# Layer 3 of a graph network: SyncE fetches one gathered column in forty-four, row by row

## The chip, the cores and the metric

The kernel runs on one core of one Trainium2 chip. The metric is the device time of one execution in microseconds. A core has four compute engines: TensorE (PE in the rows), VectorE (DVE), ScalarE (ACT) and GpSimd (POOL). A fifth engine, SyncE (SP), here only issues transfers and waits. A "q" behind a name, as in SPq, is that engine's instruction queue.

## The reference

Four graph layers run on the same graph: 3125 nodes of 64 features and 53125 edges. Each layer normalizes the features, computes something per edge from the features of its two ends, and adds it up per node. The change is in the last layer, called layer 3 here:

```python
Wh = h @ W + b
Wr = Wh[row]
Wc = Wh[col]
dot = jnp.sum(Wr * Wc, axis=-1)
sim = dot / jnp.maximum(nr * nc, EPS)      # nr, nc: the norms of Wr and Wc
prop_pos = jax.ops.segment_sum((base * relu(sim))[:, None] * Wc, row, num_segments=n_nodes)
prop_neg = jax.ops.segment_sum((base * -relu(-sim))[:, None] * Wc, row, num_segments=n_nodes)
return scale * (coeff[0] * prop_pos + coeff[1] * prop_neg + coeff[2] * Wh)
```

So each edge needs one row of a table that holds `Wh` and its norm for every node. The row is chosen by an index that is only known on the device, since the kernel sorts the edges itself.

## The kernel before

Edges and one marker entry per node (56320 places with padding) are sorted by node and laid out as 128 partitions x J = 440 columns. The columns form NBLK = 10 blocks of TB = 44. One indirect gather on GpSimd brings one column: 128 rows, one per partition, each row 130 float32 values (520 bytes) of the table `tab3`. This takes 44 gathers for a block and 440 for the layer.

`gather_blocks` (the indirect DMA is L831) issues them in order. The rows go into a ring of two slots (`ring.rows`, RING = 2). Block b uses slot b % 2. Before it refills a slot, GpSimd waits on `freed[s]`, which VectorE raises at L2835 when it has used the rows for the last time. Each gather adds 16 to the semaphore of its slot. `pieces` lists the parts that the other engines work on, with the semaphore and the count that each must reach: blocks 0 to 8 whole, then block 9 in three pieces of 24, 12 and 8 columns (LAST).

In `layer3_gather`, ScalarE waits for a part to be complete and turns its rows into a bank (`turn_rows`, L2771). VectorE runs a segmented scan over it (L2813), forms the similarities and weights (L2817 to L2832), multiplies the rows by them (L2834), frees the slot and scans again (L2837). ScalarE then packs the sums (L2784, semaphore `packed`). SyncE's whole duty in this phase is one store for each part after `packed` (L2754). ScalarE waits for the store of one part before it packs the next whole block, as there is a single buffer `sums`. `layer3_tail` then collects the sums with 25 more gathers (L2866).

The phase begins when `tab3` has been stored. SyncE does this in seven groups in `layer2_tail` (L2465), after ScalarE has finished each (`tabled`). Early in the same function VectorE rewrites the edge indices `by_src.other` as offsets into the table, counted in float32 values (L2613 to L2617).

Addresses in registers are used elsewhere in the kernel. The helper `values` (L1874) loads one or more integers from on-chip memory into an engine's registers. At L1811 SyncE uses one such value as the start of a 128-partition transfer, inside a loop of layer 1. At L1829 to L1831 TensorE's queue loads two lists of 12 values for each step.

Other transfers of SyncE whose rows are used: L1099 (97 rows of 512 bytes, on a queue that had been idle for longer than a microsecond), L1658 (67 single values, right behind L1657), L2298 and L2299 (12 rows of 512 bytes each into one partition), L2300 (one row of 512 bytes into one partition), L2190 to L2192 (64 rows of 256 bytes each), L685 (3200 single values).

Of the kernel before, what the change touches and what calls it, by code (L numbers as in the profile page):

```python
# [13 lines left out]
F32 = mybir.dt.float32  # L14
BF16 = mybir.dt.bfloat16
I32 = mybir.dt.int32
# [4 lines left out]
P = 128  # L21
N = 3125
E = 53125
NT = 25
NP = NT * P
# [6 lines left out]
TB = 44  # L32
NBLK = J // TB
RING = 2
# [15 lines left out]
R3 = 2 * (D + 1)  # L50
R3N = 3 * (D + 1)
# [28 lines left out]
SIDE = NBLK  # L80
CARRY_AT = (2, 4)
NORMED = 3


class Kern:
# [22 lines left out]
def build(nc, a, out):  # L108
    top = ExitStack()
    with top:  # L110
        K = Kern()
        K.nc, K.a, K.out = nc, a, out
        K.semaphores, K.gathers = [], []

        def sb(n, s, d=F32):
            return top.enter_context(nc.sbuf_tensor(n, s, d))

        def dram(n, s, d=F32):
            return nc.dram_tensor(n, s, d, kind="Internal").ap()


        K.ident = sb("ident", [P, P])
        K.x = sb("x", [P, NT, D])
        K.hn = sb("hn", [P, NT, D])
        K.by_src = Order("s", sb, dram)
        K.by_dst = Order("d", sb, dram)
        K.meta = sb("meta", [P, J, 2], I32)
        K.st = sb("st", [P, D])
        K.nodes = sb("nodes", [P, J])
        K.keepc = sb("keepc", [CP, SORT_W])  # L130
        K.nxc = sb("nxc", [CP, 1])
        K.nmc = sb("nmc", [CP, 2])
        K.node0c = sb("node0c", [CP, 1], I32)
        K.nodec = sb("nodec", [CP, SORT_W])
        K.base = sb("base", [P, J])
        K.co = sb("co", [P, 5])
        K.co_parts = sb("co_parts", [P, 8])
        K.item_out = sb("item_out", [1, BODIES, IBW], I32)
        K.body_w = sb("body_w", [1, BODIES], I32)
        K.item_slot = sb("item_slot", [1, BODIES, IBW], I32)  # L140
        K.item_first = sb("item_first", [1, BODIES], I32)
        K.srct = sb("srct", [P, J], I32)
        K.cid = sb("cid", [P, SORT_W], I32)
        K.pcol = sb("pcol", [P, 1], I32)
        K.iot = sb("iot", [P, NP])
        K.sums0 = dram("sums0", (L, D))
        K.sums2 = dram("sums2", (L, D))
        K.sums3 = dram("sums3", (L, D))
        K.rowsd = dram("rowsd", (P, J, RE), I32)
        K.recp = dram("recp", (L, RE), I32)  # L150
        K.pairs = dram("pairs", (SORT_L,), I32)
        K.share = dram("share", (NP,))
        K.tab1 = dram("tab1", (NP, R1))
        K.tab2 = dram("tab2", (2 * NP, R2))
        K.tab3 = dram("tab3", (NP * R3N // R3, R3))
        K.tab3n = K.tab3.rearrange("a b -> (a b)").rearrange("(n r) -> n r", r=R3N)
        K.g1 = dram("g1", (P, J, D + 1))

        with Phase(K, "ep") as ph:
            K.rows = EdgeRows(ph)  # L160
            with Phase(K, "first") as first:
                K.first = FirstList(first)
                sort_sources(K)
                layer0_pass(K)
            layer0_finish(K)
            with nc.sbuf_tensor("F", [P, H, SORT_W], F32) as K.F, \
                    nc.sbuf_tensor("item_rel", [P, ITEMS], F32) as K.item_rel, \
                    nc.sbuf_tensor("sel", [P, 4, ITEMS], F32) as K.sel:
                with nc.sbuf_tensor("atp", [P, J, 2 * H], F32) as K.atp, Phase(K, "l1g") as rows:
                    K.l1 = SourceRows(rows)  # L170
                    layer1_gather(K)
                    layer1_softmax(K)
                remaining_edges(K)
                with nc.sbuf_tensor("acc", [P, ACC_W, D + 1], F32) as K.acc, Phase(K, "l1t") as tail:
                    T = Layer1Tail(K, tail)
                    with nc.sbuf_tensor("item_ex", [P, H, ITEMS], F32) as K.item_ex:
                        layer1_spread(K, T)
                        layer1_sums(K)
                    layer1_tail(K, T)
            with nc.sbuf_tensor("wh", [P, NT, R3], F32) as K.wh:  # L180
                with Phase(K, "l2o") as ph:
                    T = Layer2Tail(K, ph)
                    layer2_gather(K, T)
                    layer2_tail(K, T)
                with Phase(K, "l3o") as ph:
                    T = Layer3Tail(ph)
                    layer3_gather(K, T)
                    layer3_tail(K, T)
# [628 lines left out]
    return bass.ds((it * size + s) * TB, TB)  # L817


def gather_blocks(nc, pool, ring, table, index, ready, last=None, axis=0):  # L820


    for b in range(NBLK):
        s, it = b % ring.size, b // ring.size
        ready(b, s, it)
        pool.sem_inc(ring.begun, 1)
        for j in range(TB):
            landed = ring.gathered[s]
            if last is not None and b == NBLK - 1:
                landed = [sem for (c, n), (sem, base) in zip(LAST, last) if c <= j < c + n][0]  # L830
            nc.gpsimd.indirect_dma_start(  # L831
                out=ring.rows[:, s, j, :], out_offset=None, in_=table,
                in_offset=bass.IndirectOffsetOnAxis(ap=index(b, s, j), axis=axis)
            ).then_inc(landed, 16)


def pieces(ring, last):

    whole = [(b, 0, TB, ring.gathered[b % RING], ring.base[b % RING] + (b // RING + 1) * TB * 16) for b in range(NBLK - 1)]
    return whole + [(NBLK - 1, c, n, sem, base + n * 16) for (c, n), (sem, base) in zip(LAST, last)]  # L840


# [1579 lines left out]
def layer2_tail(K, T):  # L2422


    nc = K.nc
    by = K.by_dst
    with Phase(K, "l2t") as ph:
        sel = ph.sb("sel", [P, NP])
        nmb = ph.sb("nmb", [P, D])
# [14 lines left out]
        made, crossed, carry, kept, joined = ph.sems("made", "crossed", "carry", "kept", "joined")  # L2444
        averaged, turned, moved, first, acted, second = ph.sems("averaged", "turned", "moved", "first", "acted", "second")
        spread, rooted, normed, turned3, moved3, third = ph.sems("spread", "rooted", "normed", "turned3", "moved3", "third")
        added, summed, tabled, stored = ph.sems("added", "summed", "tabled", "stored")
        K.tab3_stored = (stored, NG * 16)
        carry_banks = [ph.ps(f"carried{i}") for i in range(2)]
        wh = K.wh  # L2450
        C1 = D + 1
        with Step(nc, pool_ahead=True) as block:
# [7 lines left out]
            @block.sync  # L2460
            def _(sp):
                rows = lambda t: t.rearrange("(w p) r -> p w r", p=P)
                for g, (w, n) in enumerate(GROUPS):
                    sp.wait_ge(tabled, g + 1)
                    sp.dma_start(rows(K.tab3n[:, 0:R3])[:, w:w + n, :], wh[:, w:w + n, :]).then_inc(stored, 16)  # L2465
                sp.wait_ge(*K.tab3_stored)
# [128 lines left out]
            def _(dve):  # L2595
                v = nc.vector
# [18 lines left out]
                v.tensor_scalar(K.by_src.node0n[:, :], K.by_src.node0[:, :], float(R3N), None, ALU.mult)  # L2615
                v.drain()
                v.tensor_tensor(other[:, :], whole[:, 0:J], whole[:, J:2 * J], ALU.add)  # L2617
                v.drain()
                wide = lambda c, ws, n: c[:, ws].unsqueeze(2).to_broadcast([P, n, D])
                def average(t):  # L2620
                    w, n = GROUPS[t]
# [85 lines left out]
def layer3_gather(K, T):  # L2707

    nc = K.nc
    C1 = D + 1  # L2710
    with Phase(K, "l3g") as ph:
# [13 lines left out]
        blank, got, spread, masked, scanned, packed, cut_masked = ph.sems(  # L2725
            "blank", "got", "spread", "masked", "scanned", "packed", "cut_masked")
        last = [ph.gather_sem(f"last{i}") for i in range(len(LAST))]
        freed = [ph.sem(f"freed{s}") for s in range(RING)]
        out = K.sums3.rearrange("(p j) d -> p j d", p=P)
        parts = pieces(ring, last)  # L2730

        def cut(t, f, n):
            return t[:, 0:f * (n + 1)].rearrange("p (f j) -> p f j", f=f)
# [4 lines left out]
        with Step(nc, pool_ahead=True) as block:  # L2738
            @block.gpsimd
            def _(pool):  # L2740
                pool.wait_ge(*K.tab3_stored)
                nc.gpsimd.indirect_dma_start(out=first[:, :], out_offset=None, in_=K.tab3,
                                             in_offset=bass.IndirectOffsetOnAxis(ap=K.by_src.node0n[:, 0:1], axis=1)).then_inc(got, 16)
                def ready(b, s, it):
                    if it:
                        pool.wait_ge(freed[s], it)

                gather_blocks(nc, pool, ring, K.tab3, lambda b, s, j: K.by_src.other[:, b * TB + j:b * TB + j + 1], ready, last, axis=1)

            @block.sync  # L2750
            def _(sp):
                for i, (b, c0, n, landed, count) in enumerate(parts):
                    sp.wait_ge(packed, i + 1)
                    sp.dma_start(out[:, b * TB + c0:b * TB + c0 + n, :], sums[:, c0:c0 + n, :]).then_inc(stored, 16)  # L2754

            @block.scalar
            def _(act):
# [6 lines left out]
                def turn_rows(i):  # L2764
                    b, c0, n, landed, count = parts[i]
                    act.wait_ge(landed, count)
                    if i > SIDE:
                        act.wait_ge(packed, SIDE)
                    elif i and i != SIDE:
                        act.wait_ge(packed, i)  # L2770
# [20 lines left out]
            def _(dve):  # L2791
# [9 lines left out]
                for i, (b, c0, n, landed, count) in enumerate(parts):  # L2801
# [11 lines left out]
                    v.tensor_tensor_scan(flat(whole), keep, flat(whole), 0.0, ALU.mult, ALU.add)  # L2813
                    v.drain()
                    dve.wait_ge(landed, count)
                    v.tensor_copy(q[:, :], whole[:, :, n])
                    v.tensor_tensor(prod[:, 0:n, :], by_entry(whole[:, 0:D, 1:]), r[:, :, 0:D], ALU.mult)  # L2817
                    v.tensor_tensor(nn[:, 0:n], whole[:, D, 1:], r[:, :, D], ALU.mult)
# [146 lines left out]
```

## Time and profile before

| | us |
|---|---|
| median of 3 runs | 3093.05 |
| lowest, highest | 3091.59, 3096.49 |
| the profiled execution, span from first to last instruction | 3095.7 |
| GpSimd busy | 2190.4 (71%) |
| VectorE busy | 1326.6 (43%) |
| TensorE, ScalarE busy | 610.1 (20%), 481.9 (16%) |
| layer 3's 440 gathers: busy, and idle just before them | 416.1, 134.2 |

The profile gives no other time for the profiled execution than its span. Busy time does not count the issuing of transfers, register instructions and waits, so SyncE has no busy time. "Idle before" is the time in which an engine did nothing ahead of an instruction, with what ended it. "issue" means that it waited for nothing that the profile shows. The chain of waits goes back from the last instruction and asks at each step what released it.

### The profile page before, as it was taken

What the parts mean: (1) busy time and instruction counts of PE and PEld (TensorE: products, weight loads), DVE (VectorE), ACT (ScalarE), POOL (GpSimd) and SP (SyncE); (2) the same over time, 40 slices, a digit from 0 to 9 for tenths busy, and PEclk for the clock granted to TensorE, in tenths of its full rate; (3) what the DMA queues carried; (4) which work ended last, traced back from release to release, by engine and by line L of the source; (5) the groups of instructions that cost most, each with busy time, mean ns of one, the idle gap of its engine ahead of it and who ended that gap; (6) DMA issues with size and microseconds to landing.
All of it is one profiled execution on the core that took longest, in us unless ns stands there. A gap on an engine that the chain in (4) does not pass through costs nothing.

```text
span 3095.7 us, 14532 instructions
## 1 busy us (share of the span) xinstructions
PE 610.1 (20%) x3300; PEld 466.1 (15%) x3301; DVE 1326.6 (43%) x1981; ACT 481.9 (16%) x447; POOL 2190.4 (71%) x2299
## 2 busy tenths in 40 slices
PE   5521130001410000001888860000000400000001
PEld 5411110001300000001676640000000300000001
DVE  8888885202310000008466643233244615353455
ACT  2200006211100000000000022223223212111220
POOL 0177777777777777777777777777777377777774
PEclk8665565555555555555899875555555555555555
DMA  9311114212344755645355424323232123223231
GB/s 325 112 25 14 14 27 100 64 34 63 66 52 53 67 57 60 65 52 65 106 135 155 111 50 74 109 91 128 91 109 92 45 56 85 78 72 91 72 90 52
DMA packets 192274, 248.04 MB, mean 80 GB/s; under 512 B 135507, under 2 KB 146381, under 8 KB 184662
## 3 DMA queue, kind: packets, MB, share of 16 engines
q0 software_dynamic: 74048, 114.24, 19.1%
q1 hardware_dynamic: 60102, 103.67, 10.0%
q10 hardware_dynamic: 58064, 29.51, 7.9%
q14 instruction: 45, 0.37, 0.0%
q8 instruction: 15, 0.25, 0.0%
HBM read 154.17 MB, written 93.09 MB: 80 GB/s over the span
## 4 chain that ended last, share of the span: by engine, by line
POOL 55%; issue 19%; DVE 2%; ACT 0%; DMA 0%; DVEq 0%; POOLq 0%; ACTq 0%
POOL l1g_rows L831 13%; POOL l2g_rows L831 13%; POOL l3g_rows L831 12%; POOL ep_rows L1370 11%; POOL ep_rows L1351 2%; POOL l2t_res L2457 1%; POOL l3t_res L2866 1%; POOL l0f_res L1008 1%; DVE l3g_banks L2813 0%; DVE l3g_banks L2837 0%; ACT l3g_banks L2771 0%; DVE l3g_banks L2834 0%; DVE l3g_dot L2820 0%; DVEq L2819 0%; POOL ep_rows L1379 0%
## 5 line engine op out<-in xcount | busy, mean ns | idle before, releaser
L878 POOL DMA_INDIRECT l0g_rows<-in_rec_s,ents x440 | 427.4, 971 | 137.6 <-issue 133.9
L831 POOL DMA_INDIRECT l2g_rows<-tab,ep_rows x440 | 416.8, 947 | 134.2 <-issue 134.2
L831 POOL DMA_INDIRECT l1g_rows<-tab,srct x440 | 416.8, 947 | 134.2 <-issue 134.2
L831 POOL DMA_INDIRECT l3g_rows<-tab,others x440 | 416.1, 946 | 134.2 <-issue 134.2
L1370 POOL DMA_INDIRECT ep_rows<-recp,entd x352 | 338.7, 962 | 107.3 <-issue 107.3
L1572 DVE TENSOR_TENSOR l1s_A<-l1s_bank,l1s_mk 110x512 f32<-110x512 f32 x8 | 5.2, 686 | 528.4 <-PE l1s_bank L1534 528.4
L1831 PE MATMUL l1a_pa<-l1a_g,l1a_wt 128*128 x1296 | 169.6, 291 | 0.0
L1831 PEld LDWEIGHTS l1a_pa<-l1a_g,l1a_wt 128*128 128x128 f32 x1296 | 158.9, 202 | 23.8 <-issue 23.8
L2811 DVE COPY l3g_banks<-l3g_q 128x65 f32<-128x65 f32 x12 | 2.7, 229 | 306.8 <-ACT l3g_banks L2771 306.4
L2397 DVE COPY l2g_mix<-l2g_q 128x64 f32<-128x64 f32 x11 | 2.5, 228 | 306.9 <-ACT l2g_mix L2358 306.9
L1534 PE MATMUL l1s_bank<-ident,atp 128*110 128x128 f32 x64 | 10.9, 347 | 539.7 <-ACT atp L1473 530.6
L2872 PE MATMUL l3t_nmp<-ident,l3t_nmb 128*64 128x128 f32 x2 | 0.7, 447 | 575.0 <-DVEq L2889 575.0
L1847 DVE TENSOR_TENSOR l1a_wt<-l1a_place,item_ex 128x1536 f32<-128x1536 f32 x54 | 94.9, 1757 | 7.7
L1351 POOL DMA_INDIRECT ep_rows<-recp,entd x82 | 79.1, 964 | 25.0 <-issue 24.7
L319 POOL IOTA iot<- 128x3200 f32 x1 | 2.8, 2803 | 130.0 <-DVE sorts_raw L335 130.0
L1473 ACT COPY atp<-l1g_rows 128x704 f32 (+1 forms) x10 | 8.3, 826 | 552.5 <-DMA l1g_rows<-tab,srct 552.5
L1534 PEld LDWEIGHTS l1s_bank<-ident,atp 128*110 128x110 f32 x64 | 10.4, 217 | 540.4 <-issue 531.1
L2771 ACT COPY l3g_banks<-l3g_rows 128x2860 f32<-128x2860 f32 (+3 forms) x12 | 55.2, 4599 | 220.8 <-DMA l3g_rows<-tab,others 220.7
L420 DVE TENSOR_TENSOR sortd_x<-sortd_x 128x512 f32<-128x512 f32 (+1 forms) x128 | 85.6, 669 | 4.2
L2872 PEld LDWEIGHTS l3t_nmp<-ident,l3t_nmb 128*64 128x64 f32 x2 | 0.3, 203 | 575.2 <-DVEq L2889 575.2
L421 DVE TENSOR_TENSOR sortd_x<-sortd_x 128x512 f32<-128x512 f32 (+1 forms) x128 | 84.5, 660 | 0.0
L2358 ACT COPY l2g_mix<-l2g_rows 128x2816 f32<-128x2816 f32 (+2 forms) x11 | 47.5, 4318 | 231.6 <-DMA l2g_rows<-tab,ep_rows 231.6
(582 smaller groups left out, 2330.2 us busy)
## 6 DMA issues: line engine op xcount, KB each, us to landing
l1a_g<-g SPq DMA_DIRECT2D x54, 390.0 KB
recp<-ep_rows ACTq DMA_DIRECT2D x11, 1320.0 KB, 5.9
g<-l1g_rows ACTq DMA_DIRECT2D x10, 1430.0 KB, 22.7
sums<-l0s_sums SPq DMA_DIRECT2D x10, 1408.0 KB, 5.1
sums<-l2o_sums SPq DMA_DIRECT2D x9, 1408.0 KB, 4.9
sums<-l3o_sums SPq DMA_DIRECT2D x9, 1408.0 KB, 5.3
rowsd<-ep_rows POOLq DMA_DIRECT2D x8, 1452.0 KB, 5.9
ep_rows<-rowsd SPq DMA_DIRECT2D x8, 1452.0 KB, 6.6
```

The costliest lines, as they stand in the source:

```text
L420: v.tensor_tensor(out[0], pair[0], pair[1], ALU.min).then_inc(step, 1)
L421: v.tensor_tensor(out[1], pair[0], pair[1], ALU.max).then_inc(step, 1)
L831: nc.gpsimd.indirect_dma_start(out=ring.rows[:, s, j, :], out_offset=None, in_=table, in_offset=bass.IndirectOffsetOnAxis(ap=index(b, s, j ...
L878: nc.gpsimd.indirect_dma_start(out=rows[:, j, :], out_offset=None, in_=K.a["rec_s"], in_offset=bass.IndirectOffsetOnAxis(ap=K.by_src.ent[: ...
L1008: nc.gpsimd.indirect_dma_start(out=res[:, w, :], out_offset=None, in_=table, in_offset=bass.IndirectOffsetOnAxis(ap=end[:, w:w + 1], axis= ...
L1351: nc.gpsimd.indirect_dma_start(out=ring.rows[:, s, j, :], out_offset=None, in_=K.recp, in_offset=bass.IndirectOffsetOnAxis(ap=K.by_dst.ent ...
L1370: nc.gpsimd.indirect_dma_start(out=ring.rows[:, s, j, :], out_offset=None, in_=K.recp, in_offset=bass.IndirectOffsetOnAxis(ap=K.by_dst.ent ...
L1831: nc.tensor.matmul(pa[b][:, bass.ds(places[u], P)], wt[:, b, u].rearrange("p h s -> p (h s)"), g[:, b, bass.ds(slots[u], P)], start=False, ...
L1847: v.tensor_tensor(wt[:, b], place[:, b].unsqueeze(2).to_broadcast([P, IB, H, WIN]), K.item_ex[:, :, bass.ds(n * IB, IB)].rearrange("p h i ...
L2358: nc.scalar.copy(cut(bank_of(i), n)[:, :, 1:], ring.rows[:, b % RING, c0:c0 + n, D:].rearrange("p j f -> p f j")).then_inc(spread, 1)
L2457: nc.gpsimd.indirect_dma_start(out=res[:, w, :], out_offset=None, in_=K.sums2, in_offset=bass.IndirectOffsetOnAxis(ap=by.end[:, w:w + 1], ...
L2771: nc.scalar.copy(cut(bank_of(i), C1, n)[:, :, 1:], ring.rows[:, b % RING, c0:c0 + n, C1:].rearrange("p j f -> p f j")).then_inc(spread, 1)
```

## The change

In blocks 0 to 8, GpSimd leaves out the last column (SINGLE = 43), and SyncE fetches that column's 128 rows instead, each with a transfer of its own. The row's start comes from a register. Block 9 stays as it was.

In layer 2's tail, once the offsets are written (new semaphore `offset`), SyncE stores the nine columns of offsets, 1152 numbers, to DRAM. When they have landed, it loads them into one partition of an on-chip tensor `numbers`. In layer 3's gather, SyncE waits for the table and the numbers. It fetches the rows of blocks 0 and 1. Then it runs through its list of parts: ahead of the store of part i (from i = 1) it fetches the rows of block i + 1, as long as that is at most 8. From block 2 on, a fetch first waits for `freed[s]`. The rows come in groups of AT_ONCE = 8: `values` loads eight offsets into registers, then eight transfers of 520 bytes follow. Each adds 16 to `single[s]`. ScalarE and VectorE wait for 43 gathers and for 128 rows instead of for 44 gathers.

```diff
+SINGLE = TB - 1
+SINGLES = NBLK - 1
+AT_ONCE = 8
...
+def fetch_rows(K, sp, rows, table, numbers, k, most, landed):
+    for p in range(0, P, AT_ONCE):
+        begins = values(K.nc, numbers[0:1, k * P + p:k * P + p + AT_ONCE], mybir.EngineType.SP, most)
+        for i in range(AT_ONCE):
+            sp.dma_start(rows[p + i:p + i + 1, :], table(begins[i])).then_inc(landed, 16)
...
 def gather_blocks(...):
         for j in range(TB):
+            if b < singles and j == SINGLE:
+                continue
...
 layer2_tail, SyncE:
+                sp.wait_ge(offset, 1)
+                    sp.dma_start(K.numbersd.rearrange("k p -> p k"), by_src.other[:, SINGLE:SINGLES * TB:TB]).then_inc(K.numbered, 16)
+                sp.wait_ge(K.numbered, 16)
+                sp.dma_start(K.numbers[:, :], K.numbersd.rearrange("k p -> (k p)").unsqueeze(0)).then_inc(K.numbered, 16)
                 for g, (w, n) in enumerate(GROUPS):
...
 layer3_gather, SyncE:
+                def fetch(b):
+                    s, it = b % RING, b // RING
+                    if it:
+                        sp.wait_ge(freed[s], it)
+                    fetch_rows(K, sp, ring.rows[:, s, SINGLE, :], lambda n: entries[bass.ds(n, R3)].unsqueeze(0), K.numbers, b,
+                               NP * R3N - R3, single[s])
+                sp.wait_ge(*K.tab3_stored)
+                sp.wait_ge(K.numbered, 32)
+                for b in range(RING):
+                    fetch(b)
                 for i, (b, c0, n, landed, count) in enumerate(parts):
+                    if i and RING + i - 1 < SINGLES:
+                        fetch(RING + i - 1)
                     sp.wait_ge(packed, i + 1)
...
 layer3_gather, ScalarE and VectorE, beside the wait for the gathers:
+                    if i < SINGLES:
+                        act.wait_ge(single[b % RING], (b // RING + 1) * P * 16)
```

## Rows read from the trace of the kernel before

**Rows 1.** Chain of waits over layer 3's gather, shares by engine and line.

```profile
by line: POOL l3g_rows L831 65.4%; issue 27.8%; DVE l3g_banks L2813 2.3%; DVE l3g_banks L2837 2.3%; ACT l3g_banks L2771 1.5%; DVE l3g_banks L2834 1.1%; DVE l3g_dot L2820 1.1%; DVEq L2819 1.1%; ACT l3o_sums L2784 0.5%; DMA l3g_rows<-tab,othe
```

**Rows 2.** Instructions on the gathered rows: count, ns min/median/max, starts; idle time.

```profile
L831 POOL DMA_INDIRECT l3g_rows<-tab,others x440: 941/947/957, 2483.6 to 3032.6; - x147
...
  issue: 134.2, 440
...
DMA to landing us min/median/max: 2.4/2.5/5.7
```

**Rows 3.** Order in time, layer 3's gather: start us, us, engine, line, operation [idle before].

```profile
2482.30 0.95 POOL L2742 DMA_INDIRECT l3g_first<-tab,node0ns  x1 [34.54 <-issue]
...
2594.95 5.49 ACT L2771 COPY l3g_banks<-l3g_rows 128x2860 f32<-128x2860 f32 x1 [19.58 <-DMA l3g_rows<-tab,others]
2618.62 0.22 DVE L2835 COPY l3g_banks<-st 128x64 f32<-128x64 f32 x1
...
2627.99 0.32 SPq L2754 DMA_DIRECT2D sums<-l3o_sums  x1
...
2980.13 5.49 ACT L2771 COPY l3g_banks<-l3g_rows 128x2860 f32<-128x2860 f32 x1 [19.36 <-DMA l3g_rows<-tab,others]
...
3016.32 0.23 DVE L2811 COPY l3g_banks<-l3g_q 128x65 f32<-128x65 f32 x1 [5.75 <-ACT l3g_banks L2771]
...
3036.82 1.09 ACT L2771 COPY l3g_banks<-l3g_rows 128x520 f32<-128x520 f32 x1 [3.71 <-DMA l3g_rows<-tab,others]
...
3041.49 0.23 DVE L2811 COPY l3g_banks<-l3g_q 128x65 f32<-128x65 f32 x1 [0.18 <-issue]
```

**Rows 4.** One block: busy us of PE, PEld, DVE, ACT, POOL; PEclk, DMA share, GB/s.

```profile
2541.00:2596.00 55.00, 0.00 (x0) 0.00 (x0) 24.08 (x17) 10.40 (x4) 41.62 (x44) 0.50 0.30 80
```

**Rows 5.** Waits of SyncE's queue: us in total, times, longest.

```profile
SPq L2754 <- ACT l3o_sums L2784: 564.5, 12, 91.4
```

**Rows 6.** SyncE's transfer from a register's address (L1811), then its order in time.

```profile
L1811 SPq FUSED_REGOPS  x54: 37/37/51, 1513.3 to 1754.7; - x54
L1811 SPq MOVE l1a_g<-g x54: 29/29/38, 1513.4 to 1754.8; - x54
L1811 SPq DMA_DIRECT2D l1a_g<-g x54: 332/333/363, 1513.4 to 1754.8; - x54
...
1513.44 0.36 SPq L1811 DMA_DIRECT2D l1a_g<-g  x1
...
1514.29 0.34 SPq L1811 DMA_DIRECT2D l1a_g<-g  x1
```

**Rows 7.** Other transfers issued by SyncE; the last two in order of time.

```profile
L1099 SPq DMA_DIRECT2D l0m_W<-in_L_gnn_W x1: 246/246/246, 778.5 to 778.5; - x1
...
L1658 SPq DMA_DIRECT2D l1i_wst<-startdd x1: 283/283/283, 841.4 to 841.4; - x1
...
1887.09 0.86 SPq L2298 DMA_DIRECT2D wh<-share  x1
...
1888.76 0.41 SPq L2300 DMA_DIRECT2D l2o_share<-share  x1
```

**Rows 8.** Two of a series of small transfers (L2190), and their landing.

```profile
L2190 SPq DMA_DIRECT2D l2o_Wn<-in_L_gnn_W_upd x2: 466/531/596, 1862.8 to 1864.6; - x2
...
DMA to landing us min/median/max: 2.0/2.0/2.1
```

**Rows 9.** Loads of values into registers, by engine (one value; twelve values).

```profile
L1874 SPq TENSOR_LOAD <-item_first x54: 262/268/983, 1512.8 to 1751.2; - x54
L1874 PEldq TENSOR_LOAD <-item_slot x54: 846/850/2959, 1512.8 to 1760.9; - x54
```

**Rows 10.** Layer 2's tail, order in time; then the landing of 3200 single values (L685).

```profile
2419.33 0.62 DVE L2617 TENSOR_TENSOR others<-l2t_sq 128x440 int32<-128x440 f32 x1
...
2468.72 9.66 SPq L2465 DMA_DIRECT2D tab<-wh  x7
...
DMA to landing us min/median/max: 16.6/16.6/16.6
```

More of the change, by code:

```diff
@@ L155, in build @@
         K.tab3 = dram("tab3", (NP * R3N // R3, R3))
+        K.numbersd = dram("numbersd", (SINGLES, P), I32)
         K.tab3n = K.tab3.rearrange("a b -> (a b)").rearrange("(n r) -> n r", r=R3N)
@@ L179, in build @@
                     layer1_tail(K, T)
-            with nc.sbuf_tensor("wh", [P, NT, R3], F32) as K.wh:
+            with nc.sbuf_tensor("wh", [P, NT, R3], F32) as K.wh, \
+                    nc.sbuf_tensor("numbers", [1, SINGLES * P], I32) as K.numbers:
                 with Phase(K, "l2o") as ph:
@@ L817, in block_cols, with gather_blocks @@
     return bass.ds((it * size + s) * TB, TB)
-def gather_blocks(nc, pool, ring, table, index, ready, last=None, axis=0):
+def fetch_rows(K, sp, rows, table, numbers, k, most, landed):
[3 more added lines that the diff above has]
+            sp.dma_start(rows[p + i:p + i + 1, :], table(begins[i])).then_inc(landed, 16)
+def gather_blocks(nc, pool, ring, table, index, ready, last=None, axis=0, singles=0):
     for b in range(NBLK):
@@ L834, in gather_blocks, with pieces @@
             ).then_inc(landed, 16)
-def pieces(ring, last):
-    whole = [(b, 0, TB, ring.gathered[b % RING], ring.base[b % RING] + (b // RING + 1) * TB * 16) for b in range(NBLK - 1)]
+def pieces(ring, last, singles=0):
+    whole = [(b, 0, TB, ring.gathered[b % RING], ring.base[b % RING] + (b // RING + 1) * (TB - (b < singles)) * 16) for b in range(NBLK - 1)]
     return whole + [(NBLK - 1, c, n, sem, base + n * 16) for (c, n), (sem, base) in zip(LAST, last)]
@@ L2425, in layer2_tail @@
     nc = K.nc
-    by = K.by_dst
+    by, by_src = K.by_dst, K.by_src
     with Phase(K, "l2t") as ph:
@@ L2446, in layer2_tail @@
         spread, rooted, normed, turned3, moved3, third = ph.sems("spread", "rooted", "normed", "turned3", "moved3", "third")
-        added, summed, tabled, stored = ph.sems("added", "summed", "tabled", "stored")
+        added, summed, tabled, stored, offset = ph.sems("added", "summed", "tabled", "stored", "offset")
+        K.numbered, = ph.sems("numbered")
         K.tab3_stored = (stored, NG * 16)
@@ L2462, in _ @@
                 rows = lambda t: t.rearrange("(w p) r -> p w r", p=P)
+                sp.wait_ge(offset, 1)
+                with nc.allow_non_contiguous_dma(reason="one column of numbers for each of nine blocks, once"):
+                    sp.dma_start(K.numbersd.rearrange("k p -> p k"), by_src.other[:, SINGLE:SINGLES * TB:TB]).then_inc(K.numbered, 16)
+                sp.wait_ge(K.numbered, 16)
+                sp.dma_start(K.numbers[:, :], K.numbersd.rearrange("k p -> (k p)").unsqueeze(0)).then_inc(K.numbered, 16)
                 for g, (w, n) in enumerate(GROUPS):
@@ L2617, in _ @@
                 v.tensor_tensor(other[:, :], whole[:, 0:J], whole[:, J:2 * J], ALU.add)
-                v.drain()
+                v.drain().then_inc(offset, 1)
                 wide = lambda c, ws, n: c[:, ws].unsqueeze(2).to_broadcast([P, n, D])
@@ L2727, in layer3_gather @@
         last = [ph.gather_sem(f"last{i}") for i in range(len(LAST))]
-        freed = [ph.sem(f"freed{s}") for s in range(RING)]
+        freed, single = ([ph.sem(f"{n}{s}") for s in range(RING)] for n in ("freed", "single"))
         out = K.sums3.rearrange("(p j) d -> p j d", p=P)
-        parts = pieces(ring, last)
+        parts = pieces(ring, last, SINGLES)
         def cut(t, f, n):
@@ L2746, in ready @@
                         pool.wait_ge(freed[s], it)
-                gather_blocks(nc, pool, ring, K.tab3, lambda b, s, j: K.by_src.other[:, b * TB + j:b * TB + j + 1], ready, last, axis=1)
+                gather_blocks(nc, pool, ring, K.tab3, lambda b, s, j: K.by_src.other[:, b * TB + j:b * TB + j + 1], ready, last, axis=1, singles=SINGLES)
             @block.sync
             def _(sp):
+                entries = K.tab3.rearrange("a b -> (a b)")
+                def fetch(b):
[8 more added lines that the diff above has]
+                    fetch(b)
                 for i, (b, c0, n, landed, count) in enumerate(parts):
+                    if i and RING + i - 1 < SINGLES:
+                        fetch(RING + i - 1)
                     sp.wait_ge(packed, i + 1)
@@ L2815, in _ @@
                     dve.wait_ge(landed, count)
+                    if i < SINGLES:
+                        dve.wait_ge(single[s], (b // RING + 1) * P * 16)
                     v.tensor_copy(q[:, :], whole[:, :, n])
```

## The prediction

> **What bounds the kernel now.** I read the chain of waits first. Over layer 3's gather, GpSimd's indirect gathers at L831 hold 65.4% of the chain, with another 27.8% called issue [rows 1]. The issue share belongs to the same gathers: each is 0.946 us busy and preceded by 0.305 us of issue (134.2 us over 440), so one starts every 1.25 us [rows 2]. ScalarE turns block 1 at 2594.95 and block 8 at 2980.13, seven blocks at 55.03 us [rows 3]. 44 gathers of 1.251 us are 55.0 us, so GpSimd never stops between blocks. In one such block VectorE is busy 24.1 of 55 us and ScalarE 10.4, and the DMA engines 30% [rows 4]. SyncE spends 564.5 us of the phase waiting for ScalarE at L2754 [rows 5]. GpSimd's issue rate is the bound, and SyncE has almost nothing to do.
>
> The end of the phase is different. Block 8 (the ninth) is turned at 2980.13, and from there VectorE works through it and the three pieces of block 9. The last piece is turned at 3036.82 + 1.09 = 3037.9 but VectorE first takes it at 3041.49 [rows 3], so 3.6 us of slack stands there. Whatever moves the landing of block 8 moves the end by the same amount, up to that slack; GpSimd's last block moves along in both directions. I therefore count the change at one point: T8, when block 8 is complete, 2980.1 us.
>
> **What is removed.** Nine gathers of 1.251 us on the bounding engine: 11.3 us. A block takes GpSimd 43 x 1.251 = 53.8 us, and T8 by GpSimd alone becomes 2968.9.
>
> **What is added on SyncE, per row.** A transfer from an address in a register has one precedent, L1811: a FUSED_REGOPS of 37 ns, a MOVE of 29 ns, then the DMA instruction [rows 6]. Two of these transfers start 0.85 us apart (1513.44 and 1514.29) with one load between them. Of the 0.85, the DMA instruction takes 0.36, the load 0.27, the two register instructions 0.07; the remaining 0.15 us is four gaps of 0.0385. So a row costs D + 0.037 + 0.029 + 3 x 0.0385 = D + 0.182 us, where D is the DMA instruction itself.
>
> D of a one-row transfer issued after another of its kind is not in the trace. The rows near it: 0.246 us for 97 rows on an idle queue (L1099), 0.283 for 67 values right behind another transfer (L1658), 0.333 for L1811's whole tiles, and 0.411 for the only single row of about this size, 512 B at L2300. That one follows two odd transfers, the first of 0.86 us [rows 6, 7]. Behind another a transfer often takes longer than on an idle queue: L2190 issues the same form twice, first at 0.466 and in the midst of the series at 0.596 [rows 8]. I take the 0.411 as partly the queue left by its predecessors, and choose D = 0.283, between the other two and itself one that stood behind another. Bounds are 0.246 and 0.411. A row is then 0.465 us (0.428 to 0.593), and 128 rows 59.5 us (54.8 to 75.9).
>
> The Trainium skill ("DMA: Bandwidth & Descriptors", "Why a DMA increments its semaphore by 16 and not by 1") says a transfer from SyncE is spread over the largest number of engines up to 16 that divides both sides' slowest dimension, so 97 or 67 rows use one engine. A row sent as one piece would also use one, which speaks for D near those two. If the 130 values were cut instead, 13 would divide them, and the nearest price would be the 12-row transfer's 0.86.
>
> **The loads of the addresses.** One value into SyncE is 0.268 us; twelve into TensorE's sequencer 0.85 us [rows 9]. The slope is (0.849 - 0.268) / 11 = 0.053 us a value, so eight take 0.638, with a gap 0.676. Sixteen such loads per block: 10.8 us. The bounds are the one-value price (4.9 us) and the twelve-value price (14.2 us).
>
> The Trainium skill ("Runtime: NRT & Kernel Launch", "Instruction fetch mechanics") gives about 200 ns per register for loads from HBM even in bulk. Eight would be an estimated 1.6 us and sixteen loads 26 us, which would put some 139 us on the end beyond my forecast. The 71 ns per value of the twelve-value load in this trace, which reads SBUF, speaks against it, and I give it nothing of its own.
>
> **The sum.** A block on SyncE is F = 59.5 + 10.8 = 70.3 us, against 53.8 on GpSimd. SyncE becomes the bound. It starts when layer 3's table is stored, as GpSimd does, at about 2482.3 [rows 3]. It fetches blocks 0 and 1 in a row, then one block after each store. Neither of its two waits stops it when F is that long: a ring slot is freed 23.7 us after the turn began (2618.62 - 2594.95) and a block is packed and stored 33.0 us after it (2627.99), both well under F [rows 3]. GpSimd is late nowhere either: its block b+2 starts when b is freed, F - 24 us before block b+1 is complete. Seven stores lie ahead of block 8's rows at 0.36 us each, 2.5 us, and the last row lands 2.0 us after issue, as small transfers do [rows 8]. T8 = 2482.3 + 9 x 70.3 + 2.5 + 2.0 = 3119.5. That is 139 us later than 2980.1. The last block is complete in time: its slot is freed 24 us after block 7 is complete, its gathers take 55.0 + 2.5 us, and T8 is 70.3 us after block 7, so it is complete 11 us after T8, while VectorE comes to it at 3016.32, 36 us after T8 [rows 3]. So the tail keeps its length.
>
> **The other edits.** In layer 2's tail SyncE first stores the 1152 numbers and loads them back. The table of offsets is ready at 2419.33 + 0.62, and SyncE's first old duty there is at 2468.72, so 48.8 us are free. A transfer of 3200 single values landed in 16.6 us [rows 10]; by count 1152 take 6.0 and the return about 2. Even with 16.6 for each it fits, so: nothing. It could disturb GpSimd's gathers of that tail, at most for those 6 us; between 0 and +6, and I take 0. The extra waits on ScalarE and VectorE stand where both already wait for the block, and cost nothing of their own beyond T8. The row transfers move the same bytes as the gathers taken away, beside DMA engines that are 30% busy [rows 4]: 0.
>
> The profiled execution spans 3095.7 us, inside the runs' 3091.6 to 3096.5 around the median of 3093.05; I put the +139 on the median: 3232 us.
>
> **The rivals.**
> (a) SyncE keeps up. F must stay under (2980.1 - 4.5 - 2482.3) / 9 = 54.8 us to lose nothing and 53.6 to give the full gain, i.e. a row at 0.334 to 0.344 us beside loads of 10.8. That happens if a loaded register serves as the address without arithmetic: D + 0.0385 = 0.285 to 0.322, F = 47.3 to 52.0, GpSimd stays the bound and the time is 3093.05 - 11.3 = 3081.8. For it: the values in the table are already offsets in the table's entries, and TensorE's precedent needs no MOVE. Against it: L1811 does both, and entries must become bytes. 0.18, and 0.03 more for F landing between, within 0.2% of no change.
> (b) The forecast's mechanism with another price per row: one register instruction less (0.0675) gives F = 61.7 and +62 us, 3155; D = 0.246 gives F = 65.6, +97, 3190. With D = 0.333 it is F = 76.7, +197, 3290. Together with 3232 this is the forecast's own case, its range 3150 to 3300, its chance 0.59.
> (c) The one-row transfer really costs what L2300 shows, or queues behind its like. F = 75.9 + 10.8 = 86.7, T8 = 3267, +287: 3380 us. For it: it is the only row of that shape; against it: what stood in the queue ahead of it. A row cut into pieces, at the 12-row transfer's D = 0.86, would give F = 144.2 and 3897 us; the 512-byte row at L2300 did not cost that, so 0.03 of this case's chance. Time above 3300: 0.20.
>
> **Numbers.** Predicted 3232. Faster by over 0.2% (6 us, about what a measurement of this kernel tells from no change) 0.18, within it 0.03, slower 0.79. The range holds (a) and reaches into (c): 3081 to 3340, leaving out some 0.15.
>
> **What would show it.** SyncE's DMA instructions of the new line should be 1152, with starts 0.47 us apart and a load of 0.64 us after every eight. GpSimd should stop before blocks 2 to 9, released by the freeing of a slot, some 16 us a time. ScalarE's turns should come 70 us apart, released by SyncE's rows. If turns come 53.8 us apart, (a) is right. If the DMA instruction is 0.4 us or more, (c). If the turns slip while SyncE idles, or GpSimd's gathers grow beyond 1.25 us, the mechanism itself is wrong.

## The result, and the profile after

The changed kernel takes 3206.0 us (median, 3202.3 to 3207.1) against 3094.3 us before: a ratio of 1.036, with a 95% interval of 1.0345 to 1.0374. The forecast was 3232, slower.

First the page of the changed kernel: its span, and the shares of the chain that ended last. They add up to some 22% of the span, so this chain goes back about as far as the start of layer 3's gather.

```profile
span 3205.3 us, 18136 instructions
...
SPq 15%; issue 5%; DVE 1%; POOL 1%; ACT 0%; DVEq 0%; DMA 0%; POOLq 0%; ACTq 0%
```

Then the chain of waits over layer 3's gather, as in [rows 1], up to the turn of block 8:

```profile
by line: SPq L831 57.7%; issue 22.4%; SPq L1890 19.2%; ACT l3g_banks L2810 0.9%; SPq L2791 0.4%; DMA l3g_rows<-tab 0.2%; ACTq L2809 0.0%
```

The new L831 is SyncE's transfer of a row, L1890 its loads of offsets, L847 GpSimd's gather, L2810 the turn, L2791 the store of a part. GpSimd is gone from this stretch of the chain. SyncE's queue holds it from end to end: 57.7% in transfers and the register instructions on their line, 19.2% in loads.

The instructions by line (count: ns min/median/max, starts), answering to [rows 2, 6, 9]:

```profile
L831 SPq ALU_OP  x1152: 32/33/51, 2488.3 to 3088.4; - x192
L831 SPq MOVE l3g_rows<-tab x1152: 29/29/47, 2488.3 to 3088.4; - x192
L831 SPq DMA_DIRECT2D l3g_rows<-tab x1152: 224/228/925, 2488.4 to 3088.5; - x192
...
L847 POOL DMA_INDIRECT l3g_rows<-tab,others x431: 938/944/953, 2489.4 to 3101.6; - x144
...
L1890 SPq TENSOR_LOAD <-numbers x144: 698/784/1133, 2487.5 to 3084.7; - x144
```

What GpSimd waited for (us in total, times, longest):

```profile
POOL l3g_rows L847 <- issue: 129.3, 424, 0.3
POOL l3g_rows L847 <- DVE l3g_banks L2876: 77.6, 7, 14.5
```

The first of its long stops, ahead of block 4, in order of time:

```profile
2710.86 0.94 POOL L847 DMA_INDIRECT l3g_rows<-tab,others  x1 [7.07 <-DVE l3g_banks L2876]
```

GpSimd's gathers are as long as before (0.944 us against 0.947). It has nine fewer, and waits 77.6 us in all for a slot to be freed (L2876, the last use of the rows). Of the seven waits one is only 0.3 us. The six others stand ahead of blocks 4 to 9: 7.1 us the first, 13.2 to 14.5 us the later ones.

In order of time (start, us, engine, line), answering to [rows 3]: the turns of blocks 0, 1, 2 and 3 and of block 8, the handover of SyncE from one block to the next, and VectorE's first work on the last piece.

```profile
2554.44 5.49 ACT L2810 COPY l3g_banks<-l3g_rows 128x2860 f32<-128x2860 f32 x1 [63.74 <-DMA l3g_rows<-tab]
...
2618.66 5.49 ACT L2810 COPY l3g_banks<-l3g_rows 128x2860 f32<-128x2860 f32 x1 [28.66 <-DMA l3g_rows<-tab]
...
2682.83 2.19 SPq L831 DMA_DIRECT2D l3g_rows<-tab  x6
2685.07 0.36 SPq L2791 DMA_DIRECT2D sums<-l3o_sums  x1
2686.09 5.49 ACT L2810 COPY l3g_banks<-l3g_rows 128x2860 f32<-128x2860 f32 x1 [30.32 <-issue]
2686.74 2.12 SPq L831 DMA_DIRECT2D l3g_rows<-tab  x3
...
2753.61 5.49 ACT L2810 COPY l3g_banks<-l3g_rows 128x2860 f32<-128x2860 f32 x1 [31.23 <-issue]
...
3089.72 5.49 ACT L2810 COPY l3g_banks<-l3g_rows 128x2860 f32<-128x2860 f32 x1 [31.00 <-DMA l3g_rows<-tab]
...
3151.15 0.23 DVE L2850 COPY l3g_banks<-l3g_q 128x65 f32<-128x65 f32 x1 [0.18 <-issue]
```

The turns stand 64.2 us apart at first and 66.9 to 67.7 later (67.3 on average, from 2618.66 to 3089.72), where 55.03 stood before. T8 moved from 2980.13 to 3089.72, by 109.6 us. The span grew by 109.6 us too (3205.3 - 3095.7), so nothing behind T8 changed the time. From T8 to the end it is 115.6 us in both.

Layer 2's tail, answering to [rows 10], in order of time, and GpSimd's first instruction of layer 3's gather:

```profile
2419.08 0.62 DVE L2639 TENSOR_TENSOR others<-l2t_sq 128x440 int32<-128x440 f32 x1
2419.75 0.38 SPq L2482 DMA_DIRECT2D numbersd<-others  x1
...
2430.09 0.24 SPq L2484 DMA_DIRECT2D numbers<-numbersd  x1
2430.35 0.43 DVE L2647 TENSOR_TENSOR l2t_res<-l2t_res,l2t_carried 128x256 f32<-128x256 f32 x1 [10.65 <-DMA l2t_res<-sums,endd]
...
2488.14 0.95 POOL L2764 DMA_INDIRECT l3g_first<-tab,node0ns  x1 [40.78 <-issue]
```

The first work of VectorE on the gathered sums in the kernel before:

```profile
2422.79 0.42 DVE L2625 TENSOR_TENSOR l2t_res<-l2t_res,l2t_carried 128x256 f32<-128x256 f32 x1 [2.85 <-ACT l2t_carried L2549]
```

Here is something that the forecast had at nothing. The store of the 1152 offsets takes 10.3 us to land (2419.75 to 2430.09), and VectorE's first work on this tail's gathered sums waits 10.65 us for its gathers and starts at 2430.35 instead of 2422.79. Layer 3's gather begins at 2488.14, 5.8 us later than the 2482.30 of before.

### The profile page after: what moved, and what is told of

It is laid out like the page before. It is cut to its first block and busy times, and to the rows that moved or that the text cites. A ratio compares the mean times of both kernels' runs of the same rounds, so it can differ in the third digit from the quotient of the medians.

```text
span 3205.3 us, 18136 instructions
## 1 busy us (share of the span) xinstructions
PE 614.1 (19%) x3300; PEld 469.4 (15%) x3301; DVE 1326.5 (41%) x1981; ACT 481.9 (15%) x447; POOL 2176.8 (68%) x2290
## 3 DMA queue, kind: packets, MB, share of 16 engines
q1 hardware_dynamic: 63576, 104.29, 9.7%
## 5 line engine op out<-in xcount | busy, mean ns | idle before, releaser
L847 POOL DMA_INDIRECT l3g_rows<-tab,others x431 | 406.6, 943 | 206.8 <-issue 129.3
L847 POOL DMA_INDIRECT l1g_rows<-tab,srct x440 | 415.9, 945 | 134.1 <-issue 134.1
L847 POOL DMA_INDIRECT l2g_rows<-tab,ep_rows x440 | 415.5, 944 | 134.1 <-issue 134.1
L1550 PE MATMUL l1s_bank<-ident,atp 128*110 128x128 f32 x64 | 11.3, 357 | 538.6 <-ACT atp L1489 529.6
L2810 ACT COPY l3g_banks<-l3g_rows 128x2860 f32<-128x2860 f32 (+3 forms) x12 | 55.1, 4598 | 311.2 <-DMA l3g_rows<-tab 219.0
L1871 DVE TENSOR_TENSOR acc<-acc,l1a_pa 128x780 f32 x54 | 52.2, 968 | 75.3 <-PE l1a_pa L1851 75.3
```

The source lines that it names most:

```text
L847: nc.gpsimd.indirect_dma_start(out=ring.rows[:, s, j, :], out_offset=None, in_=table, in_offset=bass.IndirectOffsetOnAxis(ap=index(b, s, j ...
L1871: v.tensor_tensor(sums, sums, used[b], ALU.add).then_inc(added, 1)
L2810: nc.scalar.copy(cut(bank_of(i), C1, n)[:, :, 1:], ring.rows[:, b % RING, c0:c0 + n, C1:].rearrange("p j f -> p f j")).then_inc(spread, 1)
```

## The experiments

Each kernel was compared with the kernel before on the same chip. All but the first also move the store of the offsets, as the third does. The edits shown are against the changed kernel.

**1. The offsets alone.** The gather is that of before; only layer 2's tail keeps its edit.

```diff
-                for b in range(RING):
-                    fetch(b)
...
-                    if i and RING + i - 1 < SINGLES:
-                        fetch(RING + i - 1)
...
-                gather_blocks(..., last, axis=1, singles=SINGLES)
+                gather_blocks(..., last, axis=1)
```

> Only the edit of layer 2's tail stays: SyncE stores the 1152 offsets and loads them back. The gather is the one of before, 44 columns a block on GpSimd, and SyncE fetches no rows (it waits once more for the offsets). Theory A (the many small writes hold up GpSimd's first gathers of that tail, and the whole tail slips): about +6 us against before, 3100. Rival (the slip of the profile after is drift between two executions): 3094, no difference.

Measured: 3103.6 us against 3096.0, ratio 1.0028 (1.0018 to 1.0038), 7.6 us more. Its trace has the same late start, and the turn of block 8 (L2803) 5.9 us behind the 2980.13 of before:

```profile
2419.89 0.37 SPq L2482 DMA_DIRECT2D numbersd<-others  x1
...
2430.11 0.23 SPq L2484 DMA_DIRECT2D numbers<-numbersd  x1
2430.36 0.50 DVE L2647 TENSOR_TENSOR l2t_res<-l2t_res,l2t_carried 128x256 f32<-128x256 f32 x1 [10.53 <-DMA l2t_res<-sums,endd]
...
2985.99 5.49 ACT L2803 COPY l3g_banks<-l3g_rows 128x2860 f32<-128x2860 f32 x1 [19.25 <-DMA l3g_rows<-tab,others]
```

The slip is real, and belongs to this edit.

**2. One transfer for the column.** What the nine gathers are worth if SyncE's part costs next to nothing.

```diff
-                    fetch_rows(K, sp, ring.rows[:, s, SINGLE, :], ...)
+                    sp.dma_start(ring.rows[:, s, SINGLE, :], K.tab3[0:P, :]).then_inc(single[s], 16)
...
```

> GpSimd gathers 43 columns a block; SyncE fills the 44th of blocks 0 to 8 with one plain transfer of 128 rows of the table instead of 128 addressed rows (so the wrong rows stand in that column). The offsets are still stored and loaded, but only after layer 2's tail has received its gathers. Theory (GpSimd's issue rate is the bound and the only loss is SyncE's issue of rows): nine gathers of 1.25 us less, 3083. Rival (the last block's chain on VectorE or the two slots take the gain back): 3094.

Measured: 3084.0 against 3096.0, ratio 0.9963 (0.995 to 0.9977), 12 us less. Its turns are 53.7 us apart. The 11.3 us are there within what the interval allows, and neither the tail nor the slots take them back.

**3. The offsets later.**

```diff
                 sp.wait_ge(offset, 1)
+                for g, (w, n) in enumerate(GROUPS):
+                    sp.wait_ge(got[g], n * 16)
```

> The full change, with one move: SyncE starts the store of the offsets only when all gathers of layer 2's tail have landed. Theory A: the 6 us of the tail come back, 3200 against the change's 3206, +106 against before. Rival: no slip to remove, 3206.

Measured: 3202.1, 106 us above before (ratio 1.0343, 1.0328 to 1.0357). Its interval overlaps the change's own (1.0345 to 1.0374), so the 4 us between them are not clear by the times alone. The spans do not settle it either: this trace's is 3200.5 us, and one execution of the changed kernel had the same. What the trace shows is where the time comes back: VectorE starts at 2423.75 (L2649) for 2430.35, and T8 is at 3084.61, 5.1 us ahead of the change's. The landing times of the tail's gathers show the collision (us min/median/max), first for the change, then for this kernel:

```profile
DMA to landing us min/median/max: 2.4/2.9/10.5
```

```profile
DMA to landing us min/median/max: 2.3/2.5/3.3
```

**4. Fixed addresses.** The same 1152 transfers on the same queue, with no registers.

```diff
-        begins = values(K.nc, numbers[0:1, k * P + p:k * P + p + AT_ONCE], mybir.EngineType.SP, most)
-            sp.dma_start(rows[p + i:p + i + 1, :], table(begins[i])).then_inc(landed, 16)
+            sp.dma_start(rows[p + i:p + i + 1, :], table((p + i) * R3N)).then_inc(landed, 16)
```

> As e3_late_numbers, but the 128 transfers of a row each have fixed addresses (partition p gets row p of the table, not the row that its offset names): no loads, no address arithmetic, the same number, size and queue of transfers. Theory (SyncE's own instructions are the bound): a row costs the DMA instruction and one gap, 0.23 + 0.04 = 0.27 us, a block 34 us, under GpSimd's 53.8, so 3083. Rival (one-row transfers are bound by the DMA ring or the single DMA engine that carries them, whatever the addresses): still about 3200.

Measured: 3086.2 against 3096.0, ratio 0.997 (0.9959 to 0.9981). SyncE's transfer in its trace, and four of them in order of time with the start of the first:

```profile
L830 SPq DMA_DIRECT2D l3g_rows<-tab x1152: 212/252/1165, 2482.2 to 2934.9; - x192
...
2599.99 1.14 SPq L830 DMA_DIRECT2D l3g_rows<-tab  x4
```

Four take 1.14 us from the first start to the last end, so one every 0.29 to 0.30 us, 38 us for a block. So 1152 one-row transfers on this queue can start faster than the 0.39 us of the change; the loads and register instructions around them make the difference. One difference beside the registers was not tested apart: these rows stand one behind the other in the table, those of the change are scattered. Against it stand experiment 8, where two queues fetch scattered rows side by side without loss, and the trace after, where the instructions leave no room for a wait: 33, 29 and 228 ns and three gaps of 0.10 us together are the 0.39.

**5 and 6. Sixteen and four offsets to a load.**

```diff
-AT_ONCE = 8
+AT_ONCE = 16      # the other kernel: 4
```

> As e3_late_numbers, with 16 offsets to a load instead of 8 (8 loads a block for 16). Theory (a load has a fixed part: one value 0.27 us, eight 0.79, so 0.19 fixed and 0.074 a value): 16 values 1.38 us, loads 11.3 us a block for 13.0, nine blocks 15 us less, 3187. Rival (a load costs by the value alone, or hides behind the transfers in flight): 3202 as e3_late_numbers.

> As e3_late_numbers, with 4 offsets to a load (32 loads a block). Theory (a fixed part in each load): 4 values 0.49 us, loads 16.6 us a block for 13.0, nine blocks 32 us more, 3234. Rival (by the value alone): 3202.

Measured: 3173.6 and 3262.7 (ratios 1.0254 and 1.0541), so 28 us under and 61 us over the 3202 with eight. The direction was right and the size nearly double. The loads, sixteen first, then four:

```profile
L1890 SPq TENSOR_LOAD <-numbers x72: 1147/1234/2957, 2482.4 to 3046.5; - x72
```

```profile
L1890 SPq TENSOR_LOAD <-numbers x288: 471/556/742, 2482.3 to 3141.3; - x144
```

Between 4, 8 and 16 values a load follows 0.33 us + 0.056 us a value. The one-value load of the loop at L1811 (0.268) does not lie on that line, and it had helped to give me too small a fixed part. With a gap of 0.03, a block's loads cost 18.8, 13.0 and 10.1 us; the differences times nine are 52 and 26 us, where 61 and 28 were measured: the 28 fits, and 9 of the 61 are not explained.

**7. 112 rows.**

```diff
-    for p in range(0, P, AT_ONCE):
+    for p in range(0, 112, AT_ONCE):
...
+                    sp.dma_start(ring.rows[112:P, s, SINGLE, :], K.tab3[112:P, :]).then_inc(single[s], 16)
...
```

> As e3_late_numbers, but SyncE fetches only rows 0 to 111 by address and fills 112 to 127 with one plain transfer of table rows (so those 16 rows of nine columns are the wrong ones). Theory (the end follows nine times SyncE's time for a block as long as that is over 54.8): 14 of 16 groups, 58.9 us a block plus 0.3 for the fill, 9 x 8.1 = 73 us under e3_late_numbers, 3129. Rival (some fixed loss per block, not the count of rows): 3170 or more.

Measured: 3133.0, ratio 1.0118 (1.0102 to 1.0134); its turns of blocks 7 and 8 stand at 2957.73 and 3017.02, 59.3 us apart. That is 69 us under experiment 3 where 73 were expected. The end follows nine times SyncE's time for a block.

**8. Two issuing queues.** A version that beats both the kernel before and the change.

```diff
+CUT = 96
-    for p in range(0, P, AT_ONCE):
+    for p in range(p0, p1, AT_ONCE):
...
 SyncE: fetch_rows(..., single[s], mybir.EngineType.SP, 0, CUT)
 ScalarE, before its loop over parts:
+                act.wait_ge(*K.tab3_stored)
+                act.wait_ge(K.numbered, 32)
+                for b in range(RING):
+                    fetch(b)       # fetch_rows(K, act, ..., mybir.EngineType.Activation, CUT, P)
 ScalarE, in the loop, after the mask of the next block:
+                    if RING + i < SINGLES:
+                        fetch(RING + i)
```

> As e3_late_numbers, but SyncE fetches 96 of the 128 rows of a column and ScalarE the other 32, from its own queue: for blocks 0 and 1 at the start, for block b + 2 after it has packed block b and made the mask. Theory (the rate of one issuing queue is the bound): SyncE needs 12 of 16 groups, 12/16 of 67.3 = 50.5 us, under GpSimd's 53.8; ScalarE's 4 groups need 16 us and have some 18 free; the gathers set the pace and the time is 3084, faster than before. Rival 1 (a shared DMA engine is the bound): 3200. Rival 2 (ScalarE's loads and transfers are slower than SyncE's and delay its turn of the next block): between 3084 and 3150, with turns over 54 us apart.

Measured: 3084.1 against 3096.7, ratio 0.9961 (0.9947 to 0.9975), 12.6 us less. ScalarE between two turns, in order of time:

```profile
2592.49 5.50 ACT L2813 COPY l3g_banks<-l3g_rows 128x2860 f32<-128x2860 f32 x1 [18.02 <-DMA l3g_rows<-tab,others]
2623.11 2.51 ACT L2839 COPY l3o_sums<-l3g_banks 128x2816 f32<-128x2816 f32 x1 [25.12 <-DVEq L2899]
...
2625.76 15.71 ACTq L832 DMA_DIRECT2D l3g_rows<-tab  x28
2641.51 1.49 ACT L2801 COPY l3g_late<-keeps 128x1560 f32<-128x1560 f32 x1 [13.42 <-issue]
2646.19 5.49 ACT L2813 COPY l3g_banks<-l3g_rows 128x2860 f32<-128x2860 f32 x1 [3.19 <-DMA l3g_rows<-tab,others]
```

The turns are 53.7 us apart and released by GpSimd's gathers again; ScalarE has 3.2 us left.

**9. Half on each queue.**

```diff
-CUT = 96
+CUT = 64
```

> As e6_split, but with 64 rows for SyncE and 64 for ScalarE. Theory (ScalarE too is bound by what it issues): its 8 groups take 33 us; with the turn (5.5), the wait for VectorE (24.5), the pack (2.5) and the mask (2.6) a round of ScalarE is 68 to 69 us, over GpSimd's 53.8, so T8 slips by some 8 x 15 us and the time is about 3200. Rival (ScalarE's transfers run ahead while it waits, only the sum over the two queues counts): 3084 as e6_split.

Measured: 3171.5, ratio 1.0247 (1.0231 to 1.0263). ScalarE is the bound now: its turns of blocks 0 to 7 are 67.0 us apart on average. The last one comes after 35.8 us, because ScalarE fetches nothing more after it has packed block 6. So the 3200 was too high. T8 is 84.2 us behind that of experiment 8: 8.7 stand before the first turn (2547.57 against 2538.91), seven rounds add 13.3 us each instead of the 15 expected for eight, and the last round is 17.9 us shorter than 53.7:

```profile
3016.74 5.50 ACT L2813 COPY l3g_banks<-l3g_rows 128x2860 f32<-128x2860 f32 x1 [31.06 <-issue]
...
3052.55 5.50 ACT L2813 COPY l3g_banks<-l3g_rows 128x2860 f32<-128x2860 f32 x1
```

**10. Every other block.** SyncE alone, all 128 rows.

```diff
+ODD = (1, 3, 5, 7)
...
-            if b < singles and j == SINGLE:
+            if singles and b in ODD and j == SINGLE:
...
```

> As e3_late_numbers, but SyncE alone fetches the last column of blocks 1, 3, 5 and 7 only, all its 128 rows, and GpSimd all 44 columns of the other six. Theory (only the rate per time counts): a column takes SyncE 67 us and it has two blocks, 108 us, for it, so GpSimd's pace holds and four gathers of 1.25 us go: 5 us under before, at the edge of what can be told, with turns 53.7 and 55.0 us apart in turn. Rival (a fetch delays the block by itself, for instance by its late start after the store): 20 us or more above before.

Measured: 3090.9 against 3095.3, ratio 0.9984 (0.9975 to 0.9993), 4.4 us less, turns 53.7 and 54.9 us apart in turn. A column of 67 us does no harm where it has 108 us.

## Why the prediction was right

**The bound.** GpSimd's gathers set the pace and the nine gathers are worth 11.3 us: shown by experiment 2 (12 us less, turns 53.7 us apart).

**SyncE takes over.** F above 54.8 us turns the gain into a loss: shown from both sides, at 59.3 us (experiment 7, 36 us lost) and at three quarters of the 67 us (experiment 8, nothing lost); the 54.8 itself was not tested. With the same count of transfers but a faster issue (experiment 4), with less of the column on SyncE (experiment 8) or more time for it (experiment 10), the loss is gone; at 7/8 of the rows (experiment 7) it shrinks about as nine blocks would. Rival (a), that a loaded register serves as the address without arithmetic, was wrong: each transfer has an ALU_OP and a MOVE, 1152 of each. Rival (c), the 0.411 us of L2300 for every row, was wrong too: the rows here took 0.228. Why L2300 took 0.411 no run tested. That a row was not cut into pieces shows in the packets on the hardware queue q1: 63576 in the page of the changed kernel and 61272 in that of experiment 1, two for each of the 1152 rows.

**T8.** It moved by 109.6 us where 139 were forecast, and the tail kept its 115.6 us. The mechanism held, but the sum was made of errors of both signs:

| term | forecast | measured |
|---|---|---|
| the DMA instruction D | 0.283 us | 0.228 us |
| a row with its register instructions and gaps | 0.465 us | 0.39 us |
| 128 rows, one block | 59.5 us | 50.2 us (128 x 0.392) |
| a load of eight | 0.638 us | 0.784 us |
| 16 loads with gaps | 10.8 us | 13.0 us |
| a block with its store (from turn to turn) | 70.7 us | 67.3 us on average, the first, without a store, 64.2 us |
| layer 2's tail | 0 | +6 us |

Nine blocks at 63.2 us of rows and loads instead of 70.3 take 64 us off the 139. The later start puts 6 on. The parts of a block that no term had put 3.7 us on each of the last seven, 26 us. That gives 107; 109.6 were measured. The errors partly cancel, so it is partly luck that the total came within 30 us.

Single transfers of a row from the trace after, four in the usual order and two just behind the store of 2685.07:

```profile
2634.53 0.23 SPq L831 DMA_DIRECT2D l3g_rows<-tab  x1
2634.92 0.23 SPq L831 DMA_DIRECT2D l3g_rows<-tab  x1
2635.31 0.23 SPq L831 DMA_DIRECT2D l3g_rows<-tab  x1
2635.70 0.23 SPq L831 DMA_DIRECT2D l3g_rows<-tab  x1
...
2687.18 0.92 SPq L831 DMA_DIRECT2D l3g_rows<-tab  x1
2688.26 0.59 SPq L831 DMA_DIRECT2D l3g_rows<-tab  x1
```

The term most mis-sized is D: "I take the 0.411 as partly the queue left by its predecessors, and choose D = 0.283". The reason went the right way and not far enough: in this kernel the one-row transfer costs less (0.228) than even the 0.246 that I had as the lower bound. Rows and loads together make 63.2 us of the later 67.3. The trace shows where the other 4 us go. Two of the pieces of the chain in the block behind the store of 2685.07, the first load and a pause in front of a row's register instructions:

```profile
2685.49 1.08 SPq L1890
...
2718.64 0.35 issue
```

On average over the last seven blocks, the store with its gap is 0.4 us. The 128 DMA instructions are 1.8 us longer than 128 x 0.228, most of it in the two behind the store. The 16 loads are 0.4 us longer than 16 x 0.784, most of it in the first. Three pauses of 0.35 us, once four, make 1.1 us. The last 0.4 us are spread over the small instructions and gaps. The nine blocks have 28 such pauses, and the page of the changed kernel has 28 more packets on the queue of instructions than that of the kernel before (73 against 45). With the fixed addresses of experiment 4 it is 9 pauses and 9 more packets (54). The counts fit and suggest that SyncE pauses when its queue is refilled; no run tested it.

The Trainium skill ("Runtime: NRT & Kernel Launch", "Instruction fetch mechanics") has about 200 ns per register for loads from HBM. The loads here, from SBUF, took 98 ns a value in groups of eight (0.784 / 8), so the forecast was right to give that price nothing; no run here shows a load from HBM.

**The wrong step.** "It could disturb GpSimd's gathers of that tail [...] between 0 and +6, and I take 0." The value was the upper end: 5.8 us at the start of layer 3's gather, and 7.6 us in the times of experiment 1. The cover that I named, 48.8 us until SyncE's next duty, was there, but it hides only SyncE's wait and not what the transfer does to others. Experiment 1 shows the cost, and the trace of experiment 3 that it goes when the store comes after the gathers. I also took the landing time by count (6.0 us); it was 10.3.

**GpSimd's stops** were to be 16 us each before blocks 2 to 9. There were six, before blocks 4 to 9. The later ones are 13.2 to 14.5 us, as a block took SyncE 67.3 us and not 70.7, against 53.7 on GpSimd. Before blocks 2 and 3 the reasoning was wrong: GpSimd fills both slots without waiting, and SyncE's lag reaches it only when it has grown over some blocks. It came to block 2 at 2596.7, when the slot had been free since 2578.4 (the last use of its rows, L2876). T8 did not depend on it.

## What to carry to other kernels

Before moving work from a bounding engine to an idle one, multiply it out for one period: 128 small transfers at 0.39 us plus their loads and the store are 67 us against a period of 54, and no idle share tells this. The same work fitted once it was split over two issuing queues, or done in every other period. Where a side transfer of single values is hidden for its issuer, look at whose gathers are in flight at that time and start it after them.

## What the runs showed of the hardware

A transfer of one row from a fixed address took SyncE 0.252 us and started every 0.29 us. From a register it took 0.228 and started every 0.39: the two register instructions with their gaps add 0.10 us in all, and the DMA instruction behind them is shorter than behind its like. ScalarE's queue took 0.232 for the same transfer. A load into SyncE's registers took 0.556, 0.784 and 1.234 us for 4, 8 and 16 values, about 0.33 us + 0.056 us a value. The first load behind a store took 1.0 to 1.1 us instead of 0.784, and the second row behind it 0.9 us instead of 0.228. Some 0.35 us were lost in a pause about every 21 us, with one 8 KB packet on the instruction queue for each. A store of 1152 single values took 10.3 us to land, and the gather issued 0.01 us behind it took 10.5 us to land, where the slowest took 3.3 us when the store came later.
